# Node rows that travel with the rank scatter, a right-hand score made per step, and steps taken heavy and light by turns

## The reference, cut to what matters

```python
xn = layernorm(x)
feat = einsum('ni,rhid->rnhd', xn, conv_weights)      # 8 relations x 4 heads x 64
el = sum(feat[type, src] * attn_l[type], -1)          # one number per edge and head
er = sum(feat[type, dst] * attn_r[type], -1)
e = leaky_relu(el + er, 0.2)
alpha = softmax of e over the edges of one dst        # per head
x = x + sum over edges(alpha * feat[type, src]) + h_bias
z = layernorm(x)
gates = softmax(z @ gate_w + gate_b), the two largest kept
x = x + sum over 8 experts(gate * (gelu(z @ W1 + b1) @ W2 + b2))
```

## Time and profile before

| | |
|---|---|
| median of three runs | 1990.26 us |
| the profiled execution | 1989.72 us |
| its span | 1988.0 us |
| POOL busy | 1491.2 us (75%) |
| DVE busy | 1300.9 us (65%) |
| PE busy (matmul) | 1293.9 us (65%) |
| ACT busy | 769.2 us (39%) |
| mean granted TensorE clock | 0.813 |
| stage 1 | 0 to 309.5 us |
| stage 2, first to last gather | 312.4 to 1886.5 us |
| from the last gather to the end | 101.5 us |

### The profile page before, as it was taken

The page is one execution under the profiler, slowest core; times in us unless marked ns, Lnnn a source line. Parts: engine busy times, 40 slices in busy tenths (PEclk is TensorE's granted clock), DMA queues, the critical chain, the costliest instruction groups (busy, mean ns, idle before and its releaser), DMA issues.

```text
span 1988.0 us, 28654 instructions
## 1 busy us (share of the span) xinstructions
PE 1293.9 (65%) x6717; PEld 1027.9 (52%) x6717; DVE 1300.9 (65%) x2568; ACT 769.2 (39%) x2841; POOL 1491.2 (75%) x2229
## 2 busy tenths in 40 slices
PE   5999940003465775776666666767676768768787
PEld 2444420003354664665556565656566657657674
DVE  4643112416668876778767787877677868888881
ACT  3644410202243442334434444444444445455441
POOL 0255726878888888888888888888888888888800
PEclk9999975556786877887878787878888878888887
DMA  6465749333333333333333333333333333333400
GB/s 154 127 181 151 202 122 278 94 85 86 86 94 85 94 93 94 93 93 94 93 91 93 94 93 94 93 94 94 92 94 94 93 93 93 94 94 93 92 3 4
DMA packets 84757, 202.96 MB, mean 102 GB/s; under 512 B 30913, under 2 KB 42798, under 8 KB 80536
## 3 DMA queue, kind: packets, MB, share of 16 engines
q0 software_dynamic: 56112, 148.50, 28.0%
q10 hardware_dynamic: 9452, 33.82, 5.5%
q1 hardware_dynamic: 18980, 18.80, 3.5%
HBM read 160.51 MB, written 40.46 MB: 101 GB/s over the span
## 4 chain that ended last, share of the span: by engine, by line
POOL 46%; issue 14%; DVE 10%; PE 7%; ACT 3%; POOLq 3%; DMA 1%; DVEq 0%; ACTq 0%; SPq 0%
POOL rows L884 32%; POOL spacer L914 12%; PE y_ps L1453 4%; PE hid_ps L1439 3%; ACT rows L1365 2%; DVE rows L1049 2%; DVE fold_ps L1053 1%; DVE xo L1210 1%; POOL out_dram L892 1%; POOL node_row L901 1%; POOL xrows L884 1%; DVE rden L1038 1%; POOLq L931 1%; ACT hT L1355 1%; DVE er_hot L1006 1%
## 5 line engine op out<-in xcount | busy, mean ns | idle before, releaser
L884 POOL DMA_INDIRECT rows<-table,idx_st x982 | 947.7, 965 | 167.6 <-issue 167.1
L1453 PE MATMUL y_ps<-w,hT 128*128 128x256 f32 (+1 forms) x1920 | 524.0, 431 | 343.5 <-ACT hT L1355 343.5
L1453 PEld LDWEIGHTS y_ps<-w,hT 128*128 128x128 f32 (+1 forms) x1920 | 395.6, 213 | 435.2 <-ACT hT L1355 368.7
L1439 PE MATMUL hid_ps<-zT,w 128*128 128x128 f32 (+1 forms) x3840 | 492.7, 291 | 0.0
L1439 PEld LDWEIGHTS hid_ps<-zT,w 128*128 128x128 f32 x3840 | 484.2, 206 | 15.4 <-issue 10.8
L1355 ACT ACTIVATE hT<-hid_ps,b1t 128x128 f32<-128x128 f32 (+1 forms) x960 | 269.6, 363 | 304.6 <-PE hid_ps L1439 304.6
L1365 ACT ACTIVATE rows<-rows,ex 128x65 f32<-128x65 f32 x1320 | 326.1, 346 | 101.8 <-DVE ex L1040 101.8
L1053 DVE TENSOR_TENSOR fold_ps<-rows,fold_ps 128x780 f32<-128x780 f32 (+1 forms) x348 | 326.5, 938 | 28.3 <-DVE rows L1049 4.9
L914 POOL MEMSET spacer<- 128x280 uint8 x982 | 342.9, 349 | 0.5
L589 PE MATMUL feat_ps<-wc,xnT 128*125 128x512 f32 x480 | 221.0, 605 | 0.7 <-ACT xnT L525 0.7
L1427 PE MATMUL zt_ps<-ident,z 128*128 128x128 f32 x60 | 14.5, 330 | 279.9 <-DVE z L1157 279.9
(11 more groups left out here) (188 smaller groups left out, 1061.1 us busy)
## 6 DMA issues: line engine op xcount, KB each, us to landing
table<-stage ACTq DMA_DIRECT2D x30, 924.0 KB
rows<-table,idx_st POOLq DMA_INDIRECT x982, 2.8
w<-in_L_ffn_W_dram SPq DMA_DIRECT2D x16, 512.0 KB, 13.7
node_tab<-x_all SPq DMA_DIRECT2D x3, 1120.0 KB
table<-stage ACTq DMA_DIRECT2D x30, 107.2 KB
x_all<-in_x_dram SPq DMA_DIRECT2D x2, 1120.0 KB
wc<-_L_gnn_conv_weights_dram ACTq DMA_DIRECT2D x2, 1024.0 KB, 9.3
x_all<-in_x_dram SPq DMA_DIRECT2D x2, 560.0 KB
```

The source lines that it names most:

```text
L884: q.indirect_dma_start(buf[:, k, :], None, table, bass.IndirectOffsetOnAxis(idx[:, col + k:col + k + 1], 0)).then_inc(landed, 16)
L1439: last = t.matmul(hid_ps[e % 2][:, m * P:m * P + n], w1[:, e, k, m * P:(m + 1) * P], zT[:, k, 0:n], start=(k == 0), stop=(k == KD - 1))
L1453: last = t.matmul(y_ps[p % 2][0:n, (e % 2) * D:(e % 2 + 1) * D], hT[e % 2][:, k, 0:n], w2[:, e, k, :], start=(k == 0), stop=(k == KH - 1))
```

## The change: what it does

1. The rows of `x_all` become 264 wide. Behind the 256 features stand node, first edge, degree, and the two numbers of the layernorm (`rstd`, `nmr`). The rank scatter (now L344) writes these whole rows of 1056 B into `ranked` instead of four integers. For this a partition holds 30 neighbouring nodes, so a tile's 125 rows of `table` lie 253,440 B apart, where they were contiguous.
2. `node_tab` goes: its stores, the `residual` additions, the copy of `er` on ACT, and half of the columns of `node_scores`.
3. In stage 2 SyncE loads a step's node rows with a plain strided DMA (`load_node`), two steps ahead, as soon as `begin` has freed the buffer. ScalarE normalizes them (`node_norm`), TensorE turns them ahead of the last expert pair (`node_turn`), ScalarE copies them out of PSUM (`node_in`), TensorE makes `er` behind the last pair (`node_scores`), and `begin` reads it from PSUM and adds the bias to x.
4. `rank_sb` comes by three loads with pieces of 16 B. VectorE makes the numbers for `nb_row` before it waits for `idx_all`; before, it did this behind that wait.
5. The place of a group in the order of the steps is no longer its rank r but 2r for the first fifteen and 57 - 2r for the rest (the last one, of 38 nodes, stays last): groups 0, 28, 1, 27, 2, 26 and so on, with 40, 24, 40, 25, 40, 26 slots.
6. On TensorE the turn of the gates (`cw_turn`) now waits for `begin`.

```diff
-    node_tab = nc.dram_tensor("node_tab", (N, D + R * H), F32).ap()
-    ranked = nc.dram_tensor("ranked", (W * P, 4), I32).ap()
+    ranked = nc.dram_tensor("ranked", (W * P, XW), F32).ap()
...
-        table_v = table.rearrange("(t p r) c -> t p (r c)", t=T, p=TN)
-        x_v = x.rearrange("(t p) d -> p t d", p=TN)
+        table_v = table.rearrange("(p t r) c -> t p (r c)", t=T, p=TN)
+        x_v = x.rearrange("(p t) d -> p t d", p=TN)
...
             sp.wait_ge(ranked_out, 16 * J)
-            sp.dma_start(rank_sb[:].rearrange("p w c -> p (w c)"), ranked.rearrange("(p w) c -> p (w c)", p=P)
-                         ).then_inc(rank_in, 16)
-
-            for g in range(T // XB):
-                s = slice(g * XB, (g + 1) * XB)
-                sp.wait_ge(xb_ok, g + 1)
-                sp.wait_ge(score_free, (g + 1) * XB)
-                for a, b in parts:
-                    sp.dma_start(tab_v[a:b, s, 0:D], x_all[a:b, s, :]).then_inc(node_out, 16)
-                    sp.dma_start(tab_v[a:b, s, D:D + RH], er_all[a:b, s, :]).then_inc(node_out, 16)
-            sp.wait_ge(node_out, 2 * NP * (T // XB))
+            for i, (lo, hi) in enumerate(RANKED):
+                sp.dma_start(rank_sb[:, lo:hi, :], ranked_v.bitcast(I32)[:, lo:hi, D:D + 4],
+                             allow_slow_non_contiguous=True).then_inc(rank_in[i], 16)
...
             for j in range(J):
-                g.indirect_dma_start(ranked, bass.IndirectOffsetOnAxis(rank_u[:, j:j + 1], 0), info[:, j, :],
+                g.indirect_dma_start(ranked, bass.IndirectOffsetOnAxis(rank_u[:, j:j + 1], 0), x_all[:, j, :],
                                      None).then_inc(ranked_out, 16)
...
+            go(v.tensor_copy(rank_f[:], rank_i[:]))
+            go(v.tensor_scalar(tmpT[:], rank_f[:], -2.0, 2.0 * W - 3.0, ALU.mult, ALU.add))
+            go(v.scalar_tensor_tensor(out=rank_f[:], in0=rank_f[:], scalar=2.0, in1=tmpT[:], op0=ALU.mult, op1=ALU.min))
+            go(v.tensor_scalar(tmpT[:], rank_f[:], 0.0, float(W), ALU.is_lt, ALU.mult))
+            go(v.tensor_tensor(rank_f[:], rank_f[:], tmpT[:], ALU.add))
...
-            after(pool, begin_step, (w - 1) * N_BEGIN)
             alone(pool, pool_passed)
-            q.indirect_dma_start(node_row[par][:], None, node_tab,
-                                 bass.IndirectOffsetOnAxis(idx_st[par][:, NS:NS + 1], 0)
-                                 ).then_inc(node_landed[par], 16)
...
+        def load_node(w, par):
+            sp.dma_start(node_row[par][:], ranked.rearrange("(p w) c -> p w c", p=P)[:, bass.ds(w, 1), :]
+                         .rearrange("p o c -> p (o c)")).then_inc(node_landed[par], 16)
+        def node_ahead(w, par):
+            sp.wait_ge(begin_step, (w + 1) * N_BEGIN)
+            sp.wait_ge(xnw_ok, w + 1)
+            alone(sp, sp_passed)
+            load_node(within(w + 2) if not isinstance(w, int) else w + 2, par)
...
             dve.wait_ge(node_landed[par], (half + 1) * 16)
+            st.did(v.tensor_tensor(xres[par][:], node_row[par][:, 0:D], hb[:], ALU.add))
+            dve.wait_ge(er_ok, w + 1)
             st.did(v.tensor_copy(er9[par][:, :, 0:R].rearrange("p h r -> p r h"),
-                                 node_row[par][:, D:D + RH].rearrange("p (r h) -> p r h", r=R)))
-            st.did(v.tensor_copy(xres[par][:], node_row[par][:, 0:D]))
+                                 er_ps.rearrange("p (r h) -> p r h", r=R)))
...
-                for e in range(4, NE):
-                    gelu(u, e)
+                next_window(act, node_norm, w, par, half)
+                gelu(u, 4)
+                gelu(u, 5)
+                next_window(act, node_in, w, par, half)
+                gelu(u, 6)
+                gelu(u, 7)
...
             for p in range(PAIRS):
+                if p == 3 and turn:
+                    turn()
                 hidden(u, 2 * p, n)
                 hidden(u, 2 * p + 1, n)
                 if p == 0:
+                    if turn:
+                        pe.wait_ge(begin_step, (u + 2) * N_BEGIN)
                     cw_turn(u)
                 second(u, p, n)
                 if p == 0:
                     b2_term(u)
+                if p == 3 and scores:
+                    scores()
```

More of the change, by code:

```diff
@@ L273, in phase1 @@
         NP = 16 * len(parts)
+        starts_at = {lo: i for i, (lo, hi) in enumerate(RANKED)}
         def group_of(i):
@@ L488, in _ @@
             v.tensor_copy(nb_f[:], nb_i[:]).then_inc(nbf_ok, 1)
-            residual(2)
+            dve.wait_ge(idx_in, 16 * W)
+            go(v.tensor_scalar(low, idx_all[:].bitcast(I32), R - 1, None, ALU.bitwise_and))
+            go(v.scalar_tensor_tensor(out=late, in0=late, scalar=float(R), in1=low, op0=ALU.mult, op1=ALU.add))
+            go(v.tensor_scalar(typ_all[:], late, float(R), None, ALU.min))
             dve.wait_ge(nb_tr, 2)
@@ L833, in _ @@
         w2_v = W2.rearrange("e (k p) n -> p e k n", p=P)
+        for i in range(2):
+            sp.dma_start(node_row[i][:], ranked.rearrange("(p w) c -> p w c", p=P)[:, i, :]).then_inc(node_landed[i], 16)
         for e in range(NE):
@@ L1307, in stage @@
         def stage(w, par):
[L1309 to L1313 removed]
+            a.copy(idx_st[par][:], idx_all[:, bass.ds(w, 1), 0:NS].rearrange("p o k -> p (o k)")
+                   ).then_inc(idx_staged, 1)
         def xstage(w, par):
@@ L1339, in den_of_window, with node_norm, node_in @@
             den_of(w, diff, diff_ok, th, th_ok, den, den_ok)
+        def node_norm(w, par, half):
+            act.wait_ge(node_landed[par], (half + 1) * 16)
+            after(act, xtr_ok, w)
+            a.activation(xnw[:], node_row[par][:, 0:D], ACT.Identity, bias=node_row[par][:, D + 4:D + 5],
+                         scale=node_row[par][:, D + 3:D + 4]).then_inc(xnw_ok, 1)
+        def node_in(w, par, half):
+            act.wait_ge(xtr_ok, w + 1)
+            after(act, er_ok, w)
+            a.copy(xnwT[:], xt_ps.rearrange("p (k n) -> p k n", k=KD)).then_inc(xnwT_ok, 1)
         def z_in(u):
@@ L1408, in window @@
             bt.leave(w, nb, g)
+        node_norm(0, 0, 0)
+        node_in(0, 0, 0)
         windows(act, window)
@@ L1432, in z_turn, with node_turn, node_scores @@
             last.then_inc(logit_ok, 1)
+        def node_turn(w, par, half):
+            pe.wait_ge(xnw_ok, w + 1)
+            for k in range(KD):
+                last = t.transpose(xt_ps[:, k * P:(k + 1) * P], xnw[:, k * P:(k + 1) * P], ident[:])
+            last.then_inc(xtr_ok, 1)
+        def node_scores(w, par, half):
+            pe.wait_ge(xnwT_ok, w + 1)
+            after(pe, begin_step, w * N_BEGIN)
+            for k in range(KD):
+                last = t.matmul(er_ps, xnwT[:, k, :], wa[:, k, RH:2 * RH], start=(k == 0), stop=(k == KD - 1))
+            last.then_inc(er_ok, 1)
         def hidden(u, e, n=P):
@@ L1480, in window @@
                 z_turn(u)
-                experts(u)
-        pe.wait_ge(const_in, 64)
+                experts(u, P, lambda: next_window(pe, node_turn, w, par, half),
+                        lambda: next_window(pe, node_scores, w, par, half))
+            else:
+                node_turn(w + 1, 1 - par, half + par)
+                node_scores(w + 1, 1 - par, half + par)
+        pe.wait_ge(const_in, 80)
+        node_turn(0, 0, 0)
+        node_scores(0, 0, 0)
         pe.wait_ge(w_in, 16 * NE)
```

116 lines of the change are left out of this document (58 added, 58 removed).

## The result

The changed kernel takes 1946.2 us (median of four runs, 1943.5 to 1951.2), the kernel before 1990.5 us beside it: a ratio of 0.9784 [0.9769, 0.9799]. In a later comparison it took 1949.2 us against 1989.9, 0.9802 [0.9788, 0.9815]. So it is 2% faster, inside the predicted range, but 11 to 14 us short of the 1935 us that the sum gave. The profiled execution took 1945.0 us (span 1943.3).

A forecast was written before the change was run, and what follows sets the result against it. The prediction took POOL's gather pace to bound stage 2, with one 17.0 us PE wait in stage 1. It summed 1989.7 - 25.5 (earlier first gather) - 36.3 + 5 + 2 = 1934.9, said 1935 us, range 1914 to 1960.

The forecast's parts named there:

- Stage 1: Setup stage: PE's 17.0 us wait for `nb_f` and 1.7 us slow restart go; stores end another 5.5 us sooner without `node_tab`.
- The index chain: End of stage 1: chain ready 5 us later, DVE's last operations ending about 275, 7 us of cover, no cost.
- Rival (a): Index chain comes late: 20 us later gives 1948 us, 35 later gives 1965; chance 0.12.
- rival (b): Table stores to rows 253,440 B apart take twice their time: 1958 us; chance 0.06.
- Part 3: Node gather leaves POOL: first gather comes sooner, and 29 others save 1.25 us each, 36.3 us.
- The output scatters: Stage 2: scatters in steps 4 and 6 wait for late outputs, 5.5 us each, where 6 to 7 were: plus 5.
- The order and the end: New step order avoids losing some 9 of 36 us in the last four steps, but does not shorten the end.
- The 101.5 us stay: Behind the last gather: the time in which PE, DVE and ACT finish the last two steps stays the same.
- The 2 us that the new work of PE and DVE should cost at the end: Last two steps: transposes, narrow products and `begin` have nothing to hide them; plus 2 us, bounds 0 and 5.
- rival (c): Step loop becomes the bound through the new relay between ACT, PE and DVE: 2047 us at 10 us a step; chance 0.03.

The follow-up runs named there:

- b_nb_early: Kernel before with only the edge-type operations and their wait for all edge entries put behind the nb numbers on DVE: 1971.3 us, 0.9905.
- second run: The changed kernel measured again without edits, for a second profile of its end: 1949.2 us.
- e_wait_behind: Changed kernel with the wait for the last step's spacers moved behind the first row gather of a step: 1928.0 us, 0.9687.
- b_turns: Kernel before with only the order of the steps changed to heavy and light by turns: 1985.5 us, 0.9971.
- falling order: Changed kernel with the steps in the old order, from the highest degrees to the lowest: 1951.7 us, 0.9803.
- e_dummy: Changed kernel with one small gather into an unread buffer put back on POOL where the node gather stood: 1955.9 us, 0.9823.
- b_wait_behind: Kernel before with the spacer wait moved behind a step's first row gather: 2374.9 us against 2311.6, on a slower chip; repeated, 2152.2 against 2116.2.
- e_best: Changed kernel with the spacer wait behind a step's first row gather and the output scatter behind gather 16 instead of 8: 1912.3 us, 0.9616.

## Why the prediction was right, and where it was 11 to 14 us off

The measured time lies in the range, and most of the mechanism is as predicted. That it lies as near as 11 to 14 us is partly luck: one term was 26 us too large, and the others, each of them a little too slow, gave 14 to 16 back, 5 of them in the first profile by the clock alone.

**Stage 1: right.** The wait of 17.0 us and the restart were counted as 18.7 and are 18.6 (b_nb_early). What the end of the `node_tab` stores and the first node gather give on top was counted as 6.8; the first gather is 6.9 us sooner in the changed kernel than in b_nb_early (292.9 to 286.0), and 7.7 in the second run.

**The index chain: hidden, with less cover than I said.** The scatters took 1190 ns as taken, the landing 7.1 us in place of 3.4, and DVE's last operations began 10.8 us later than before and not 5. They end at 281.3; the last packet of the table's stores ends at 283.5, and ACT enters stage 2 at 284.35. Of the 7 us of cover about 2 were left. Rival (a) was right in its direction and stayed inside the cover.

**The strided stores: rival (b) is wrong.** A packet of 8448 B took 342 ns before and 337 ns after between 160 and 215 us (medians of the packets). The share of the store queue rose from 44.9 to 50.5% with the larger scatters beside it, at 7.06 MB for 7.54, about 1.2 times the engine time per byte; PE has no wait there for a free stage buffer, ACT four short ones (2.2 us in sum). The pitch is not the reason for the 1.2: from 60 to 160 us, ahead of the scatters, the queue of the table's stores takes the same time per byte in both kernels, before and after:

```profile
q10 hardware_dynamic: 1958, 13.58, 41.7%
q10 hardware_dynamic: 1936, 13.42, 41.2%
```

The Trainium skill ("DMA: Bandwidth & Descriptors", "Latency and other measured facts") has a clear loss only from a pitch of 2 MiB on, 164 GB/s where 207 are reached at 512 KiB; at 253,440 B these packets agree.

**Part 3, the step that failed: "29 stand within POOL's line: 29 x 1.25 = 36.3 us".** The time between two starts in the earlier trace rows was read as the price of the gather. It was the pace of a line in which the 0.8 us between the spacer wait and the row gather passed in the node gather's shadow. The passages gave 9.5 to 10.5 us: 0.5 at each start without the branch, nothing in the mean at those behind it, and about 1.2 only at the first start and the three with extra gathers. When the wait stands behind a gather again, they give 36.1 (e_wait_behind). The mechanism (POOL is the bound, the gather goes) was right, the size of this term was a quarter of what I said. The hint stood in the earlier trace rows: the gap ahead of the row gather behind the node gather was 0.31 us, ahead of every other one 0.17. A wait stood there and nearly nothing of it could be seen.

**The output scatters: right in kind, smaller.** They wait in steps 4 and 6 and nowhere else, 4.1 us each and not 5.5: 2.2 us more than before, not 5.

**The order and the end.** "The 101.5 us stay" was wrong. In the new order alone the end is 3.6 us shorter (b_turns), since `er_hot` of the last step is no longer as late; in the changed kernel it is 12.3 to 12.5 us behind the last gather, where the falling order would have 20.7. The prediction had 9 us for that order; the traces say 8 at that place, the medians 2.5 to 5.5. The 2 us that the new work of PE and DVE should cost at the end can't be seen: from `er_hot` of the last step to the end are 86.8 us before, and in the changed kernel 79.7 (granted clock 0.90) and 85.0 (0.83), in the falling order 83.0. Its 104.6 us from the last gather, 2.1 more than before, come from the later `er_hot`. Between the changed kernel's two profiles the end differs by 5 us by the clock alone, so no single one can price a term of 2 us.

**The step loop: rival (c) is wrong.** `e_diff` to the next `er_hot` took 43 to 44 us in heavy steps and 36 to 41 in light ones (before 40 to 44 and 35 to 41), and POOL waits for nothing of it in the middle. From the changed kernel's timeline of DVE, a heavy step:

```profile
1003.13 0.33 DVE L1041 TENSOR_TENSOR e_diff<-ebuf,m_win 128x160 f32<-128x160 f32 x1
...
1047.15 1.66 DVE L1018 TENSOR_TENSOR er_hot<-fold_ps,hot 128x1440 f32<-128x1440 f32 x1
```

Summed up against the predicted span of 1933.3: passages +25.8 to +26.8, scatters -2.8, other gaps -0.6 to -3.1, the end -6.2 to -11.4, first gather -0.9 to -1.7: +10 and +12.8 for the two profiles.

**Open:** why a start behind the loop's branch took 3.4 us in the kernel before and 2.75 with the small gather of e_dummy. The traces say where the time goes: the sequencer comes late to the register work of the new step. The load of its step counts from `nb_row` starts 0.0 to 0.8 us behind `space_end` in the changed kernel (at most of the other starts 5.3 ahead of it), 0.6 to 1.2 ahead in the kernel before and 2.1 to 2.5 ahead in e_dummy. Why it moves by so much they don't say. Open as well: what ACT waited for on the two slower chips; and what the edit of b_wait_behind does to the time where POOL is the bound.

## What to carry to other kernels

Before you book a removed instruction at the distance between its start and the next one's, ask what in the queue passes while it runs: a wait behind it becomes visible when it goes, and then the place of that wait is worth more than the instruction. Waits that have long been met cost nothing here, also directly ahead of an indirect DMA. What costs is a wait of an engine for its own last instruction, because it keeps the sequencer from preparing the next one: put such a wait behind an indirect DMA where the data allow it, not ahead of it. And look for single long waits of an engine in the setup stage: one order on VectorE was worth 18.6 us here, nearly twice what 29 removed gathers gave.

## What the runs showed of the hardware

- An indirect DMA of GpSimd behind a wait that only the memset just before it could meet started 0.92 us behind that memset, and 0.76 to 0.80 us behind the sequencer's last record; with the wait one instruction later, 0.16 us behind the memset (changed kernel, e_wait_behind). The memset behind the moved wait lost nothing.
- Long-met waits directly ahead of gathers 16, 20, 24 and 30 of a step cost nothing: 1.46 us from gather to gather as elsewhere (changed kernel). GpSimd's sequencer passed the one ahead of gather 16 as gather 10 started.
- A scatter of 1056 B per row cost GpSimd 1188 ns (median), one of 16 B 1187 ns; only the landing grew, from 3.4 to 7.1 us.
- Stores of 8448 B packets to rows 253,440 B apart took the same engine time per byte as to contiguous ones (60 to 160 us: 41.2% for 13.42 MB, 41.7% for 13.58); beside scatters of 1056 B rows it was 1.2 times as much as beside those of 16 B.
- The 3840 reads of 16 B that bring back `rank_sb` took 9 ns each (median), all of them within 222.1 to 226.0 us.
- The kernel before took 1990 to 1992 us on two chips and 2116 and 2312 us on two others. In the three profiles taken on the slower two, of edits, ScalarE stands in 62 to 71 waits, 279 to 456 us from 462 to 1800 us, that no record explains; in e_best's profile there is none.
